# One graph layer on one core: the issuing engine's program for the edge loop written out group by group, with one address load for two groups

## What is computed

```python
def _mlp(h, W, b, gamma, beta):
    h = relu(h @ W + b)
    mu, var = mean(h, axis=0), mean(square(h - mu), axis=0)
    return gamma * (h - mu) * rsqrt(var + EPS) + beta

h = maximum(_layernorm(x), 0.0)                       # (6250, 96)
node_feat = _mlp(h, W_node, ...)                      # (6250, 96)
edge_feat = _mlp(edge_attr, W_edge, ...)              # (100000, 96) from 4 columns
message = concatenate([h[src], h[dst], edge_feat])    # (100000, 288)
message = _mlp(message, W_msg, ...)                   # (100000, 96)
return x + segment_sum(message, dst) + node_feat
```

## Time and profile before

| | |
|---|---|
| median of 3 runs | 1119.44 us |
| the profiled execution, its own time | 1120.07 us |
| its span, from the first to the last instruction | 1118.3 us |
| edge loop: SP's first load of it to the last | 253.3 to 1092.6 us |
| PE busy | 781.5 us (70%) |
| POOL busy | 750.8 us (67%) |
| DVE busy | 544.2 us (49%) |
| ACT busy | 369.7 us (33%) |
| mean granted TensorE clock | 0.87 |

### The profile page before, as it was taken

One profiled execution on the slowest core, in us unless ns is written; L12 is line 12 of the kernel. 1 busy time (PEld: TensorE's weight loads), 2 busy tenths in 40 slices (PEclk: granted clock), 3 DMA queues, 4 the chain that ended last, 5 costly groups with the idle time before them and its releaser, 6 DMA issues.

```text
span 1118.3 us, 22745 instructions
## 1 busy us (share of the span) xinstructions
PE 781.5 (70%) x4800; PEld 635.8 (57%) x4800; DVE 544.2 (49%) x1401; ACT 369.7 (33%) x620; POOL 750.8 (67%) x786
## 2 busy tenths in 40 slices
PE   3416966626777767776777777767788777777778
PEld 3315722215666656665666666656677665666664
DVE  8778799983333333333334334333343333334335
ACT  4614988842222222222222222222222222222220
POOL 6877777777777777777777777777777777730000
PEclk9758988876899898889889889898887889889899
DMA  9655333352222222222222222222232222221113
GB/s 286 212 190 127 92 87 86 87 141 59 63 62 61 61 64 61 61 62 63 62 60 63 62 61 61 62 62 62 61 63 62 61 61 64 62 43 22 25 21 89
DMA packets 93984, 87.01 MB, mean 78 GB/s; under 512 B 65445, under 2 KB 70069, under 8 KB 93832
## 3 DMA queue, kind: packets, MB, share of 16 engines
q0 software_dynamic: 25024, 38.49, 16.1%
q1 hardware_dynamic: 68352, 47.05, 15.8%
q10 hardware_dynamic: 584, 1.22, 0.3%
HBM read 68.80 MB, written 14.54 MB: 75 GB/s over the span
## 4 chain that ended last, share of the span: by engine, by line
SPq 54%; issue 21%; DVE 10%; PE 7%; ACT 5%; DMA 3%; ACTq 0%; DVEq 0%
SPq L438 28%; SPq L435 20%; DVE edge_st L941 4%; SPq L431 3%; ACT r_sb L577 3%; SPq L416 2%; PE pc L670 2%; DMA big_a<-zeros 1%; DMA xs<-x_stack 1%; PE pa L695 1%; PE pc L762 1%; PE pd L773 1%; DVE ln_buf L856 1%; DVE ring L877 1%; SPq L273 1%
## 5 line engine op out<-in xcount | busy, mean ns | idle before, releaser
L466 POOL DMA_INDIRECT ring<-p_table,src_idx x734 | 693.5, 945 | 223.8 <-issue 197.6
L773 PE MATMUL pd<-hm 128*97 128x193 f32 x1564 | 341.4, 368 | 0.0
L773 PEld LDWEIGHTS pd<-hm 128*97 128x97 f32 x1564 | 281.0, 191 | 9.8
L762 PE MATMUL pc<-w3q,r_sb 128*128 128x96 f32 x1564 | 245.7, 307 | 13.9 <-DMA w3q<-q_table 7.7
L762 PEld LDWEIGHTS pc<-w3q,r_sb 128*128 128x128 f32 x1564 | 218.2, 216 | 20.3 <-issue 9.7
L741 PE MATMUL pa<-xs,we_stack 128*128 128x512 bf16 x196 | 83.4, 426 | 204.3 <-DMA xs<-x_stack 204.1
L615 ACT ACTIVATE r_sb<-pa 128x512 f32<-128x512 f32 x196 | 116.8, 596 | 326.6 <-PE pa L741 323.8
L1004 DVE TENSOR_SCALAR hm<-pb 128x384 f32<-128x384 f32 x196 | 109.1, 557 | 222.6 <-PE pb L747 195.5
L625 ACT ACTIVATE hm<-pc 128x384 f32<-128x384 f32 x196 | 96.3, 491 | 312.2 <-DVE pc L1015 304.2
L1015 DVE TENSOR_TENSOR pc<-pc,ring 128x384 f32<-128x384 f32 x196 | 110.8, 565 | 97.9 <-PE pc L762 91.5
L741 PEld LDWEIGHTS pa<-xs,we_stack 128*128 128x128 bf16 x196 | 20.6, 105 | 235.2 <-issue 219.8
(11 more groups left out here) (112 smaller groups left out, 360.9 us busy)
## 6 DMA issues: line engine op xcount, KB each, us to landing
w3q<-q_table SPq DMA_DIRECT2D x782, 11.2 KB
ring<-p_table,src_idx POOLq DMA_INDIRECT x734
xs<-x_stack SPq DMA_DIRECT2D x98, 72.0 KB
x_stack<-ring SPq DMA_DIRECT2D x6, 980.0 KB, 7.5
xs<-x_stack SPq DMA_DIRECT2D x98, 60.0 KB
ring<-in_x_nodes SPq DMA_DIRECT2D x5, 480.0 KB, 8.8
big_a<-zeros SPq DMA_DIRECT2D x1, 2400.0 KB, 13.4
p_table<-ring SPq DMA_DIRECT2D x12, 192.0 KB
```

What stands on the lines that cost most here:

```text
L466: nc.gpsimd.indirect_dma_start(out=ring[:, tile * C:(tile + 1) * C], out_offset=None, in_=table, in_offset=bass.IndirectOffsetOnAxis(ap=id ...
L762: last = nc.tensor.matmul(pc[:, j % 2, t * C:(t + 1) * C], r_sb[:, j % 2, t * TILE:(t + 1) * TILE], w3q[:, j, t, :], start=True, stop=True)
L773: last = nc.tensor.matmul(pd[0:M1, j % 2, 0:HW], hm[:, j, t, WIN:HW], hm[:, j, t, :], start=(t == 0), stop=(t == n - 1))
```

## The change

Only SP's program in the edge loop changes. The hardware loop goes: the 196 groups are written out one after the other, as POOL's program is already, so each address, buffer and semaphore value that depended on the loop counter becomes a constant. The nodes are read once for two groups, eight at a time, ahead of the wait of the first of the two, and the check at run time that each node is below N goes. The loads, their sizes, their order and their semaphores stay.

```diff
             with sp.If(outside < 1):
-                def fast(i):
-                    for j in range(BODY):
-                        g = num(i, j)
-                        if j % 2 == 0:
-
-                            wait(sp, hot_lin, g - 2)
-                            sp.dma_start(xs[0:KX, j // 2, :], x_stack[:, bass.ds(g * GROUP, 2 * GROUP)]).then_inc(
-                                x_main[j // 2], 16)
-
-                        wait(sp, pre_summed, g - 3)
+                for g in range(NG):
+                    i, j = at(0, g)
+                    if g % 2 == 0:
+
+                        wait(sp, hot_lin, g - 2)
+                        sp.dma_start(xs[0:KX, j // 2, :], x_stack[:, g * GROUP:(g + 2) * GROUP]).then_inc(
+                            x_main[j // 2], 16)
                         _, at_node = nc.values_load_multi_w_load_instructions(
-                            bases[0:1, bass.ds(g * TPG + NG, TPG)], [mybir.EngineType.SP], min_val=0, max_val=N - 1)
-                        for t in range(tiles(i, j)):
-                            sp.dma_start(w3q[M1:M1 + TWIN, j, t, :], q_table[bass.ds(at_node[t], TWIN), :]).then_inc(
-                                q_in[j], 16)
-                    load_res(i)
-                passes(sp, fast)
+                            bases[0:1, NG + g * TPG:NG + (g + 2) * TPG], [mybir.EngineType.SP], min_val=0,
+                            max_val=N - 1,
+                            skip_runtime_bounds_check_because="a node of an edge, below N by the kind of input")
+
+                    wait(sp, pre_summed, g - 3)
+                    for t in range(tiles(0, g)):
+                        sp.dma_start(w3q[M1:M1 + TWIN, j, t, :],
+                                     q_table[bass.ds(at_node[g % 2 * TPG + t], TWIN), :]).then_inc(q_in[j], 16)
+                    if j == BODY - 1:
+                        load_res(i)
```

## The result

The changed kernel takes 1019.54 us (median of 4 runs, 1019.37 to 1019.70), the kernel before beside it 1119.99 us. The ratio is 0.9105, with a 95% interval of 0.9089 to 0.9121: 100 us or 9% faster.

What follows compares the result with a forecast made beforehand. SP's issue in the edge loop bounds the kernel; relieved, POOL's last gather does. Products of group 194 at 996.4 plus 26.0 us of end plus 1.5 for slow clock give span 1023.9, hence 1025.0 us; range 1020 to 1044.

Steps and rivals of the forecast that it cites:

- SP bounds the kernel before: Edge loop before: SP's own instructions, mainly node reads and tile loads, were over half the chain of waits.
- SP's new price, 5.3 us a pair: SP's edge loop, two groups: 0.42 xs, 0.55 nodes, 4.1 tile loads, half a res load; 5.3 us instead of 8.6.
- PE 2.8 us a fed step, POOL met after 280 us at 535 us: Edge loop: PE uses a group in 2.8 us, POOL supplies one in 5.0; its 44-group lead lasts 280 us.
- POOL sets the end and keeps its pace: Edge loop's end: set by POOL's last gather, unchanged at 991.7 us; nothing added for denser traffic, or 37 us as bound.
- The end, from the last gather to the last instruction: After POOL's last gather: group 194's products start at 996.4, plus 26.0 us is 1022.4; with 1.5 for slow clock, 1023.9.
- From the span to the median: Whole run: execution 1.8 us above its span and 0.6 us above the median, taking span 1023.9 to 1025.0 us.
- A: Rival, edge loop: PE's own steps average above 3.8 us through half-speed clock; 1051 us, up to 1119; chance 0.06.
- B: Rival, edge loop: SP stays the bound, needing over 7.6 us a pair; 1070 us at 8.1; chance 0.04.
- C: Rival, POOL's gathers: slowed by the denser traffic; up to 1062 us; chance 0.02.
- D: Rival, SP's written-out issue: tile loads cost up to 1.18 us instead of 0.33; 1460 us, slower than before; chance 0.03.
- E: Rival, SP in the chain only because it was last to be seen; the old time stays; chance 0.01.

Runs made afterwards that it cites:

- AHEAD = 8: The changed kernel with POOL announcing a group after issuing the gathers of the group eight later instead of three, with twelve landing semaphores: 1022.75 us, ratio 0.9137.

## Why the prediction was right or wrong

- **SP bounds the kernel before; its cost lies in L435 and L438.** Right. That the check at run time alone holds the whole gain I had not seen, because I priced the nodes' part as one lump of 1.62 us; the rows of the register work and the checks were in the trace.
- **SP's new price, 5.3 us a pair.** Undersized: 5.69 in the mean. Of the 0.4 us, the load of eight nodes has 0.27: 0.784 us and a gap of 0.03, in place of 0.55. One register took 0.486 and four 0.464, and I drew a flat line from that to eight; behind register work eight take 0.694, and directly behind a transfer's issue a load takes 0.08 to 0.09 us more in the median, which 8 of the 196 loads in the trace before showed. The rest is 0.1 us in the eight tile loads and under 0.1 us of gaps. It cost nothing in the end, since SP had slack up to 7.6 us.
- **PE 2.8 us a fed step, POOL met after 280 us at 535 us.** 2.85 us, and 577 us. The number is right by luck. I had SP get ahead at 2.65 us a group and wait, and PE set the pace; SP never got ahead, and the pace was its own 2.84 us. PE, where it has groups to work off at full clock (the end of the run with AHEAD = 8), takes 2.63 us a step. The lead is not 44 but 47 groups, since a group is announced when it has landed and not three groups later.
- **POOL sets the end and keeps its pace.** Right: last gather at 992.1, forecast 991.7. The two runs with gathers left out show both that it is the bound now (838 us) and that it wasn't before (1121 us).
- **The end, from the last gather to the last instruction.** This is the step that failed: "Group 191 is announced at 990.1, 192 to 193 at 992.6". From it I had 194 in its products at 996.4, which puts the last group's sum at 999.7 (in the timeline before, that sum, at 1095.59, stands 22.7 us ahead of the end). The step takes the source's order for the time of the chip: it lets the announcement wait until the gathers of three later groups are carried out, and so leaves PE several groups to work off behind POOL. POOL's record after has the announcement of 191 at 977.06 us, 13 us earlier, and 192 to 195 at 982.62, 987.20, 992.05 and 995.30, each 2.5 to 3.2 us after the start of its own last gather. Nothing is left to work off: the products of 194 start at 986.55, and the last sum, at 995.42, waits for the landing of the last gather alone (3.2 us after its start at 992.06). That is 4.3 us of the 6.3 by which the span was missed. The rest: 1.5 us that I had added for a slow clock in the two steps ahead, and 0.5 us in the end itself, 22.2 us against 22.7.
- **From the span to the median.** I added 1.1 us (1.8 less 0.6), as in the runs before. After, the median stands 1.9 us above the profile's span of 1017.6, so 0.8 us go the other way: 6.3 - 0.8 = 5.5 us, from 1025.0 to 1019.5.
- **The range.** Its lower end of 1020 allowed an end 4 us shorter than the sum but not that a stated delay of three groups is none at all. The bound from below was there to be had: the last gather's start, its shortest landing (counted from the start) and the way from the last sum to the end, 991.65 + 2.4 + 22.7 + 1.1 = 1017.9 us.
- **Rivals.** A did not come: the granted clock was 0.98 up to 577 us, and the slow steps in the later part were hidden, PE being idle there for 28% of the time. Of B, the written-out program does cost a little, 0.3 us every 128 instructions, under 0.1 us a pair, far from the 2.3 us a pair that B needed; in the run that keeps the check, and with it SP as the bound, the 33 gaps are about 10 us of its 1083. C, D and E fell: the slowest tile load after is 0.761 us.

## What to carry to other kernels

When a queue's own instructions fill the chain of waits, price them one by one: here the check on each value read at run time cost 0.25 us, 784 times, and leaving it out alone was worth as much as the whole change. That rests on the premise that every node is below N, which nothing tests at run time any more. Before you count the gain, find the producer that is slower than the present rate but has a lead; its last item plus the tail is the new time, however much the first engine is relieved. And where a program announces work some steps late, look in the trace at when the consumer really starts, instead of adding up the steps of the source.

## What the runs showed of the hardware that was not expected

- POOL's queue ran 11 gathers ahead of the gather being carried out: with 32 gathers between a group and its announcement in the program, the announcement came when 21 of them had started, 26.2 us after the group's last gather.
- Reading registers on SP costs by their number and by what stands directly ahead. Behind register work: 0.464 us for four and 0.694 for eight. Directly behind the issue of a transfer: 0.541 and 0.784. Eight registers directly behind another reading: 0.52. The rule of about 200 ns for each register in the Trainium skill (Runtime: NRT & Kernel Launch, Instruction fetch mechanics) gives 1.6 us for eight. This trace does not agree: its longest usual row for eight, 0.784 us, is half of that.
- Written-out code on SP has a gap of about 0.3 us after every 128 recorded instructions (33 times in one run, 20 in another), where the hardware loop has no such row of gaps. Each gap is followed within 1.5 us by one 8192-byte packet of the queue of kind "instruction". The same section of the Trainium skill says that crossing a block of 16 KiB, 256 instructions, is mostly hidden. The trace agrees that it is small, but its step is 128 instructions and 8 KiB, half of what the section gives. That the transfer is what makes SP pause is not shown.
